# A two-layer graph network with h on the stationary side in layer two: the mean joins the product on VectorE, and TensorE transposes the sum

## The chip, the cores and the metric

The kernel runs on one core of one Trainium2 chip. The metric is the device time of one execution in microseconds (us). Engines are called by their names or as the profile does: TensorE (PE for matmuls, PEld for its weight loads), VectorE (DVE), ScalarE (ACT), GpSimd (POOL) and SyncE (SP), which only starts transfers here.

## The reference, cut to what matters

There are 12,500 nodes with 256 features each and 200,000 edges, sorted by their destination `dst`.

```python
def _sage_conv(x, src, dst, W_l, b_l, W_r):
    msgs = x[src]
    agg = segment_sum(msgs, dst, num_segments=N_NODES)
    deg = segment_sum(ones, dst, num_segments=N_NODES)
    mean = agg / maximum(deg, 1.0)[:, None]
    return mean @ W_l + b_l + x @ W_r

h = relu(_sage_conv(x, src, dst, W1_l, b1, W1_r))
h = relu(_sage_conv(h, src, dst, W2_l, b2, W2_r))
x = layernorm(x + (h @ W3 + b3))
```

## The kernel before, in words

The destinations are cut into 100 **windows** of 125 nodes (`WN`), and the edges into blocks of 128, four blocks to a **group**. Because the product with `W_l` is linear, layer one ends by writing `z = h @ W2_l` to HBM (`z_dram`), and layer two sums rows of z instead of rows of h. It also writes h itself, transposed, one window to a piece of 128 partitions by 250 columns (`h_dram`).

In each layer GpSimd runs through 304 groups. For each it starts four gathers (line 429, 128 rows of 256 numbers each) into one of the four slots of `ring`. It may overwrite a slot once TensorE has read the first three blocks of the group that lay there four groups ago (`s_gr`), and for the fourth gather once the third block of the next group has been read. VectorE marks for each group which of its 128 edges of a block belong to which node of the window (`oh`, line 940), and TensorE multiplies marks by rows (line 516), four blocks to a **pair**, into one of three banks of `psA`. VectorE adds the result two pairs later into `acc` (line 918). A group whose edges reach into a second window takes one more pair. Five heavy windows get part of their edges by another way: their counts are multiplied by all rows in order (`dense_step`, line 587), and VectorE adds that sum once in four groups (`add_hot`, line 1040), which I call the hot addition.

Behind the second and the fourth group of each four, `finish_one` lets each engine close one window i of layer two if its edges are done. Each engine comes to that place in its own program:

- VectorE, `dense2(i)`: scales the sum to the mean (line 1106), loads a register for the next window, computes one reciprocal for the norm of an earlier window (line 1100), and goes on to the next group's marks.
- TensorE, `dense2(i)`: first `product3(i)`, which is the output product of window i-1 (lines 664 and 666), then for each half m of 128 columns the two products of the weights W2_r with the transposed h (line 678, the weights stationary, h moving with 125 columns) and on top of them the transposed mean, made by a product with the identity (line 682), both in `psT`.
- ScalarE, `relu_t(i)`: waits for that, takes bias and relu into `tT` (line 1283); then `norm(i-2)` (line 1314) and `center(i-1)` (lines 1303 to 1308), and the transfers of x and h for later windows.

The order of all work is written out by hand in each engine's program; semaphores alone tie the engines together. `s_T2` counts TensorE's finished windows, `s_t2` VectorE's means, `s_tc2` ScalarE's.

The last three windows close together at the end (`finish`), behind the last group.

Of the kernel before, what the change touches and what calls it, by code (L numbers as in the profile page):

```python
# [22 lines left out]
N, E, D = 12500, 200000, 256  # L23
P = 128
WN = 125
NW = N // WN
# [121 lines left out]
def build(nc, x, src, dst, W1l, b1, W1r, W2l, b2, W2r, W3, b3, c_f, c_s, c_win, c_node, out):  # L148
# [5 lines left out]
    with ExitStack() as ctx:  # L154
# [6 lines left out]
        def sem(name):  # L161
            return ctx.enter_context(nc.semaphore(name))
# [21 lines left out]
        xt, mean, zb, sq, y = (work[:, a:a + n] for a, n in (  # L184
            (0, 2 * D), (2 * D, D), (3 * D, 2 * D), (6 * D, D), (7 * D, D)))
# [19 lines left out]
        psH, psZ = psY[:, 0:512], psY[:, 512:]  # L205
        psS = ps4[:, 2 * 512:].rearrange("p (k n) -> p k n", k=2)
# [70 lines left out]
        s_hd, s_hx = sem("s_hd"), sem("s_hx")  # L277

        s_x2, s_t2, s_T2, s_tc2, s_M3, s_y, s_act, s_sd, s_rs, s_o = (
            sem(n) for n in ("s_x2", "s_t2", "s_T2", "s_tc2", "s_M3", "s_y", "s_act", "s_sd", "s_rs", "s_o"))  # L280
# [154 lines left out]
        def _(pe):  # L435
# [234 lines left out]
            def dense2(i):  # L670
                with pe.If(i > 0):
                    product3(i)
                q = pe.snap((i & 1) * 2 * WN)
                pe.wait_ge(s_hx, i * 16 + 16)
                pe.wait_ge(s_tc2, i + 1)
                for m in range(2):
                    for k in range(2):
                        pe.matmul(psT[:, m * WN:(m + 1) * WN], w2[:, k, D + m * P:D + (m + 1) * P],  # L678
                                  hT[:, bass.ds(q + k * WN, WN)], start=(k == 0), stop=False)
                    if m == 0:  # L680
                        pe.wait_ge(s_t2, i + 1)
                    mm = pe.matmul(psT[:, m * WN:(m + 1) * WN], mean[0:WN, m * P:(m + 1) * P],  # L682
                                   ident[0:WN, 0:WN], start=False, stop=True)
                mm.then_inc(s_T2, 1)
# [78 lines left out]
        def _(v):  # L763
# [338 lines left out]
            def dense2(i):  # L1102
                at = sums()
                v.wait_ge(s_ad[1], v.snap(c, min_val=1, max_val=NG * NW + 2))
                v.wait_ge(s_T2, i + 1)
                v.tensor_scalar(mean[0:WN, :], acc[0:WN, bass.ds(at, D)],
                                rdeg[0:WN, bass.ds(i, 1)], None, ALU.mult).then_inc(s_t2, 1)
                next_range(i)
                with v.If(i > 1):
                    inverse(i)  # L1110
# [94 lines left out]
        def _(act):  # L1205
# [59 lines left out]
            def load_h(i):  # L1265
                act.dma_start(hT[:, i % 2 * 2 * WN:(i % 2 + 1) * 2 * WN], h_dram[i]).then_inc(s_hx, 16)
# [10 lines left out]

            def relu_t(i):
                act.wait_ge(s_T2, credit[s_T2] + i + 1)
                if i >= 1:  # L1280
                    act.wait_ge(s_M3, i)
                for m in range(2):
                    ins = act.activation(tT[:, m, :], psT[:, m * WN:(m + 1) * WN], ACT.Relu, bias=b2c[:, m:m + 1])  # L1283
                ins.then_inc(s_tc2, 1)
                if i + 2 < NW:
                    act.wait_ge(s_hx, 16 * (i + 2))
                    load_h(i + 2)
# [8 lines left out]
            def center(j):  # L1296
# [6 lines left out]
                link(act.activation(sq[0:WN, :], py, ACT.Copy, accum_out=sm[0:WN, 0:1]))  # L1303
# [3 lines left out]
                link(act.activation(sq[0:WN, :], y[0:WN, :], ACT.Square, accum_out=var[0:WN, :]))  # L1307
                act.activation(sd[0:WN, :], var[0:WN, :], ACT.Sqrt, bias=eps[0:WN, :], scale=1.0 / D).then_inc(s_sd, 1)

            def norm(j):  # L1310
                act.wait_ge(s_rs, j + 1)
                if j >= 2:
                    act.wait_ge(s_od[j % 2], 16 * (j // 2))
# [11 lines left out]
            act.wait_ge(s_hx, 16)  # L1325
            load_h(1)
            for i in range(NW + 2):
# [33 lines left out]
```

## Time and profile before

| | |
|---|---|
| median of 3 runs | 3268.58 us (3262.19 to 3272.46) |
| span of the profiled execution | 3265.6 us |
| PE, PEld busy | 2761.8 us (85%), 2310.7 us (71%) |
| DVE, ACT, POOL busy | 1460.5 us (45%), 498.3 us (15%), 2381.1 us (73%) |
| layer two, first to last gather | 1685.94 to 3239.04 us |

The span runs from the first to the last instruction of one execution; the page gives no other time for that execution, and the median lies 3.0 us above its span. Busy shares say how much of the span an engine computed; GpSimd's share leaves out the time in which it issues a gather. The matmul ends are modelled, so one matmul's duration in a group is longer than the step from one to the next.

### The profile page before, as it was taken

The numbers are of one execution on the slowest core, as the hardware profiler recorded it, in microseconds if no ns is written. First come the engines' busy times: TensorE is split into PE (matmuls) and PEld (weight loads), VectorE is DVE, ScalarE is ACT, GpSimd is POOL, SyncE is SP. The second block draws the span as 40 slices with busy tenths as digits, with TensorE's granted clock in tenths as the row PEclk, the third lists the DMA queues.
The fourth block names the chain that finished last, engine by engine and source line by source line (L and its number), as shares of the span: only waits on it lengthen the run. The fifth ranks groups of instructions, "written<-read, shape, count | busy, mean of one in ns | idle before, by whom it ended". The sixth has DMA issues, their size and how long they took to land.

```text
span 3265.6 us, 61269 instructions
## 1 busy us (share of the span) xinstructions
PE 2761.8 (85%) x13183; PEld 2310.7 (71%) x13184; DVE 1460.5 (45%) x3301; ACT 498.3 (15%) x1511; POOL 2381.1 (73%) x2439
## 2 busy tenths in 40 slices
PE   4888889899899899889867778878988978978877
PEld 3556778787787788678755667767777867867765
DVE  5676656666555555433333333333333333333332
ACT  2000111110110111011110121112122112212113
POOL 4757777777777777767747777777777777777775
PEclk7989999999999999899988889999989999999998
DMA  4334678587687677777755657757757757757743
GB/s 115 116 118 147 177 246 253 173 254 248 182 254 234 205 245 239 238 234 218 212 174 173 190 169 227 222 166 227 222 170 228 227 167 222 230 168 227 218 128 108
DMA packets 495815, 650.77 MB, mean 199 GB/s; under 512 B 184190, under 2 KB 414453, under 8 KB 492502
## 3 DMA queue, kind: packets, MB, share of 16 engines
q0 software_dynamic: 116736, 318.92, 32.7%
q1 hardware_dynamic: 298166, 253.95, 25.4%
q10 hardware_dynamic: 80800, 76.82, 7.8%
q14 instruction: 95, 0.78, 0.1%
q8 instruction: 18, 0.29, 0.0%
HBM read 579.07 MB, written 70.40 MB: 199 GB/s over the span
## 4 chain that ended last, share of the span: by engine, by line
PE 32%; POOL 28%; issue 17%; DVEq 9%; DMA 7%; DVE 5%; ACT 1%; SPq 1%; ACTq 0%; PEldq 0%; PEld 0%; POOLq 0%
POOL ring L429 28%; PE ps L516 19%; PE ps L587 5%; DMA ring<-z_rows,scol 4%; PE psY L631 2%; DMA ring<-in_x,scol 2%; DVEq L928 2%; PE psY L620 1%; PE psB L561 1%; DVE oh L986 1%; DVE acc L918 1%; PE psY L664 1%; DVE oh L940 1%; PE psT L678 1%; DVEq L948 1%
## 5 line engine op out<-in xcount | busy, mean ns | idle before, releaser
L516 PE MATMUL ps<-ring,oh 128*125 128x257 f32 (+1 forms) x6384 | 1606.2, 404 | 370.5 <-DMA ring<-z_rows,scol 185.7
L516 PEld LDWEIGHTS ps<-ring,oh 128*125 128x125 f32 x6384 | 1237.4, 199 | 650.0 <-issue 455.6
L429 POOL DMA_INDIRECT ring<-in_x,scol x1216 | 1196.8, 984 | 461.0 <-issue 348.4
L429 POOL DMA_INDIRECT ring<-z_rows,scol x1216 | 1183.8, 973 | 397.3 <-issue 356.0
L940 DVE SCALAR_TENSOR_TENSOR oh<-dcol,cf,iota 128x500 f32<-128x500 int16 x798 | 591.6, 741 | 630.5 <-issue 315.0
L918 DVE TENSOR_TENSOR acc<-ps,acc x802 | 338.5, 422 | 589.7 <-PE ps L516 404.7
L587 PE MATMUL ps<-scratch 128*125 128x257 f32 (+1 forms) x2000 | 476.5, 385 | 7.9 <-DMA scratch<-counts 4.8
L587 PEld LDWEIGHTS ps<-scratch 128*125 128x125 f32 x2000 | 454.2, 294 | 22.4 <-issue 6.6
L1283 ACT ACTIVATE work<-psT,b2c 128x125 f32<-128x125 f32 x200 | 62.2, 363 | 1194.1 <-PE psT L682 1194.1
L1247 ACT COPY work<-psY 125x256 f32<-125x256 f32 x100 | 37.2, 372 | 1273.6 <-PE psY L620 1273.6
L561 PE MATMUL psB<-oh 128*128 (+1 forms) x546 | 159.8, 393 | 63.8 <-DVE oh L986 60.4
L631 PEld LDWEIGHTS psY<-work,w 128*128 128x128 f32 x1600 | 198.8, 195 | 7.2 <-issue 1.1
L986 DVE TENSOR_SCALAR oh<-iota,cf,key 128x500 int16 (+1 forms) x546 | 202.0, 411 | 0.0
L631 PE MATMUL psY<-work,w 128*128 128x125 f32 x1600 | 198.3, 278 | 0.8 <-issue 0.8
L561 PEld LDWEIGHTS psB<-oh 128*128 (+1 forms) x546 | 50.8, 97 | 150.8 <-issue 118.6
L620 PE MATMUL psY<-w,hT 128*125 128x256 f32 x400 | 112.2, 405 | 14.6 <-issue 13.0
L1024 DVE COPY scratch<-psB 128x500 f32 x125 | 84.9, 679 | 82.5 <-issue 77.7
L678 PE MATMUL psT<-hT,w 128*128 x800 | 121.7, 274 | 0.1
L983 DVE TENSOR_TENSOR oh<-iota,key 128x256 int16 (+1 forms) x273 | 114.1, 418 | 9.6 <-PE psB L561 7.3
L678 PEld LDWEIGHTS psT<-hT,w 128*128 128x128 f32 x800 | 113.1, 191 | 6.5 <-issue 0.5
L664 PE MATMUL psY<-w,work 128*125 128x256 f32 x400 | 107.5, 392 | 3.1 <-ACT work L1283 2.6
L620 PEld LDWEIGHTS psY<-w,hT 128*125 128x125 f32 x400 | 74.8, 197 | 43.8 <-issue 28.1
(120 smaller groups left out, 1100.5 us busy)
## 6 DMA issues: line engine op xcount, KB each, us to landing
scratch<-counts SPq DMA_DIRECT2D x200, 312.5 KB
scratch<-in_x SPq DMA_DIRECT2D x114, 512.0 KB
scratch<-z_rows SPq DMA_DIRECT2D x114, 512.0 KB
counts<-scratch SPq DMA_DIRECT2D x25, 1250.0 KB, 8.8
work<-in_x ACTq DMA_DIRECT2D x200, 125.0 KB
ring<-in_x,scol POOLq DMA_INDIRECT x1216
ring<-z_rows,scol POOLq DMA_INDIRECT x1216
scratch<-in_x SPq DMA_DIRECT2D x114, 128.0 KB
```

What stands on the lines that cost most here:

```text
L429: pool.indirect_dma_start(ring[:, slot, b, 0:D], None, rows_dram, bass.IndirectOffsetOnAxis(scol[:, n - C0:n - C0 + 1], 0)).then_inc(rows[ ...
L516: mm = pe.matmul(psA[0:WN, bass.ds(bank, W)], oh[:, R if later else slot, b, :], ring[:, slot, b, 0:W], start=(b == 0), stop=(b == nb - 1))
L561: mm = pe.matmul(psB[:, 0:n], oh1[:, bass.ds(at, P)], oh1[:, bass.ds(at + P, n)], start=first and b == 0, stop=True, skip_group_check=True)
L587: mm = pe.matmul(psD[0:WN, 0:W], lin_a[:, q, :, :, k].rearrange("p f n -> p (f n)"), lin_x[:, q, k, 0:W], start=(q == 0 and k == 0), stop= ...
L620: mm = pe.matmul(psZ[0:WN, 0:D], hT[:, k * WN:(k + 1) * WN], w2[:, k, 0:D], start=(k == 0), stop=(k == 1))
L631: mm = pe.matmul(psH[:, m * WN:(m + 1) * WN], w1[:, a, k, m * P:(m + 1) * P], tT[:, 2 * a + k, :], start=(a == 0 and k == 0), stop=(a == 1 ...
L664: pe.matmul(at, tT[:, k, :], w3[:, k, :], start=(k == 0), stop=False)
L678: pe.matmul(psT[:, m * WN:(m + 1) * WN], w2[:, k, D + m * P:D + (m + 1) * P], hT[:, bass.ds(q + k * WN, WN)], start=(k == 0), stop=False)
L918: v.tensor_tensor(at, psA[0:WN, bass.ds(v.snap(par, min_val=0, max_val=(BANKS - 1) * 512), W)], at, ALU.add).then_inc(s_ad[l], 1)
L940: v.scalar_tensor_tensor(out=ohf[:, at:at + nb * WN].rearrange("p (b n) -> p b n", n=WN), in0=dcol[:, bass.ds(blk, nb)].unsqueeze(2).to_br ...
L983: v.tensor_tensor(s[:, :, 0:P], iota[:, 0:P].unsqueeze(1).to_broadcast([P, 2, P]), key[:, 0, bass.ds(at, 2)].unsqueeze(2).to_broadcast([P, ...
L986: ins = v.tensor_scalar(s[:, b, P:P + n], iota[:, table:table + n], base, key[:, 1, bass.ds(at + b, 1)], ALU.add, ALU.is_equal)
```

## The change

Layer two no longer streams h through stationary weights. ScalarE copies window i's h from `hT` into the free half of `tT` (`copy_h`), TensorE takes that copy as the stationary side of a product 256 columns wide, the result of which (125 nodes by 256 columns, `psU`) lies in the bank `psB`, VectorE computes acc times 1/deg plus psU in one instruction, and TensorE transposes this sum in its two halves. The scratch tile `sq` goes, since its place is now used by the copy of h; its two users write to `y` and `zb`.

```diff
+        psU = psB[0:WN, 0:D]
...
             def dense2(i):
+                pe.wait_ge(s_hc, i + 1)
+                for k in range(2):
+                    mm = pe.matmul(psU, tT[:, 2 + k, :], w2[:, k, D:2 * D], start=(k == 0), stop=(k == 1))
+                mm.then_inc(s_U, 1)
                 with pe.If(i > 0):
                     product3(i)
-                q = pe.snap((i & 1) * 2 * WN)
-                pe.wait_ge(s_hx, i * 16 + 16)
                 pe.wait_ge(s_tc2, i + 1)
+                pe.wait_ge(s_t2, i + 1)
                 for m in range(2):
-                    for k in range(2):
-                        pe.matmul(psT[:, m * WN:(m + 1) * WN], w2[:, k, D + m * P:D + (m + 1) * P],
-                                  hT[:, bass.ds(q + k * WN, WN)], start=(k == 0), stop=False)
-                    if m == 0:
-                        pe.wait_ge(s_t2, i + 1)
-                    mm = pe.matmul(psT[:, m * WN:(m + 1) * WN], mean[0:WN, m * P:(m + 1) * P],
-                                   ident[0:WN, 0:WN], start=False, stop=True)
+                    mm = pe.transpose(psT[:, m * WN:(m + 1) * WN], mean[0:WN, m * P:(m + 1) * P], ident[0:WN, 0:WN])
                 mm.then_inc(s_T2, 1)
...
                 v.wait_ge(s_T2, i + 1)
-                v.tensor_scalar(mean[0:WN, :], acc[0:WN, bass.ds(at, D)],
-                                rdeg[0:WN, bass.ds(i, 1)], None, ALU.mult).then_inc(s_t2, 1)
+                v.wait_ge(s_U, i + 1)
+                v.scalar_tensor_tensor(out=mean[0:WN, :], in0=acc[0:WN, bass.ds(at, D)],
+                                       scalar=rdeg[0:WN, bass.ds(i, 1)], in1=psU, op0=ALU.mult,
+                                       op1=ALU.add).then_inc(s_t2, 1)
                 next_range(i)
...
+            def copy_h(i):
+                act.wait_ge(s_hx[i % 2], 16 * (i // 2 + 1))
+                if i >= 1:
+                    act.wait_ge(s_U, i)
+                act.copy(tT[:, 2:4, :].rearrange("p a n -> p (a n)"),
+                         hT[:, i % 2 * 2 * WN:(i % 2 + 1) * 2 * WN]).then_inc(s_hc, 1)
+                if i + 2 < NW:
+                    act.wait_ge(s_hc, i + 1)
+                    load_h(i + 2)
+
             def relu_t(i):
+                if i + 1 < NW:
+                    copy_h(i + 1)
                 act.wait_ge(s_T2, credit[s_T2] + i + 1)
...
                 ins.then_inc(s_tc2, 1)
-                if i + 2 < NW:
-                    act.wait_ge(s_hx, 16 * (i + 2))
-                    load_h(i + 2)
...
-                link(act.activation(sq[0:WN, :], py, ACT.Copy, accum_out=sm[0:WN, 0:1]))
+                link(act.activation(y[0:WN, :], py, ACT.Copy, accum_out=sm[0:WN, 0:1]))
...
-                link(act.activation(sq[0:WN, :], y[0:WN, :], ACT.Square, accum_out=var[0:WN, :]))
+                if j >= 2:
+                    act.wait_ge(s_od[j % 2], 16 * (j // 2))
+                link(act.activation(zb[0:WN, (j % 2) * D:(j % 2 + 1) * D], y[0:WN, :], ACT.Square,
+                                    accum_out=var[0:WN, :]))
```

On TensorE, this is one window's place in layer two before the change, from the last matmul of `product3` on. Every row is one instruction or several alike; `work` holds the mean and `tT`, `w` the weights, and what stands in brackets are the semaphores waited for.

```order
L666 MATMUL psY<-work,cf 125x256
L671 UNCONDITIONAL_BRANCH
L674 ISA
L675 REGISTER_ALU [waits s_hx]
L678 REGISTER_ALU [waits s_tc2]
L678 ISA
L678 MATMUL psT<-hT,w 128x125
L678 ISA
L678 MATMUL psT<-hT,w 128x125
L682 MATMUL psT<-cf,work 128x125 [waits s_t2]
L678 MATMUL psT<-hT,w 128x125 x2
L682 MATMUL psT<-cf,work 128x125
```

The same place after the change (its line 675 is the new product, 666 and 668 are `product3`, 682 the transposes):

```order
L675 MATMUL psB<-w,work 125x256 [waits s_hc]
L675 MATMUL psB<-w,work 125x256
L677 COMPARE_AND_BRANCH
L666 REGISTER_ALU [waits s_y,s_tc2]
L666 ISA
L666 MATMUL psY<-w,work 125x256 x2
L667 REGISTER_ALU
L668 ISA [waits s_x2]
L668 MATMUL psY<-work,cf 125x256
L677 UNCONDITIONAL_BRANCH
L682 MATMUL psT<-cf,work 128x125 [waits s_t2,s_tc2]
L682 MATMUL psT<-cf,work 128x125
```

The product with h has moved ahead of `product3`, and what follows `product3` is now two transposes that wait for VectorE.

On VectorE, the same window before the change, from the wait for the last addition to the reciprocal:

```order
L1105 REGISTER_ALU [waits s_ad1]
L1106 ISA [waits s_T2]
L1106 TENSOR_SCALAR work<-acc,rdeg 125x256
L1079 ISA
L1079 TENSOR_LOAD tables
L1109 COMPARE_AND_BRANCH
L1100 REGISTER_ALU [waits s_sd]
```

And after it:

```order
L1104 REGISTER_ALU [waits s_ad1]
L1106 ISA [waits s_U,s_T2]
L1106 SCALAR_TENSOR_TENSOR work<-acc,rdeg,psB 125x256
L1078 ISA
L1078 TENSOR_LOAD tables
L1110 COMPARE_AND_BRANCH
L1099 REGISTER_ALU [waits s_sd]
```

Nothing has moved here, but the instruction now waits for TensorE's product of the same window, and the reciprocal, the hot addition and the next marks stand behind it.

On ScalarE, one window early in layer two before the change, from the relu to the first instruction of `center`:

```order
L1283 ACTIVATE work<-psT,b2c 128x125 [waits s_M3,s_T2]
L1283 ACTIVATE work<-psT,b2c 128x125
L1266 DMA hT<-h_cols 128x250 [waits s_hx]
L1212 DMA work<-in_x 125x256 [waits s_x2,s_M3]
L1303 ACTIVATE work,sm<-psY 125x256
```

And after it (1283 is now the copy, 1267 the load of h, 1296 the relu, 1313 in `center`):

```order
L1283 COPY work<-hT 128x250 [waits s_U,s_hx0]
L1267 DMA hT<-h_cols 128x250 [waits s_hc]
L1296 ACTIVATE work<-psT,b2c 128x125 [waits s_M3,s_T2]
L1296 ACTIVATE work<-psT,b2c 128x125
L1213 DMA work<-in_x 125x256 [waits s_x2,s_M3]
L1313 ACTIVATE work,sm<-psY 125x256
```

The load of h has moved from behind the relu to ahead of it, behind the new copy.

## Rows read from the trace of the kernel before

**Rows 1.** The page's first line: the span of the profiled execution.
```profile
span 3265.6 us, 61269 instructions
...
```

**Rows 2.** Groups by line, layer two (1700 to 3266 us): busy us, mean ns, idle before.
```profile
...
L429 POOL DMA_INDIRECT ring<-z_rows,scol x1205 | 1173.0, 973 | 367.2 <-issue 352.9 <-PE ps L516 14.3
L516 PE MATMUL ps<-ring,oh 128*125 128x256 f32 x3186 | 821.1, 411 | 254.7 <-DMA ring<-z_rows,scol 170.8 <-DVE oh L940 40.9 <-DVE acc L918 31.0
...
L682 PE MATMUL psT<-cf,work 125*128 125x125 f32 x400 | 77.3, 275 | 0.0
...
L1314 ACT ACTIVATE work<-work,rs 125x256 f32<-125x256 f32 x100 | 50.6, 506 | 0.5 <-DVE rs L1100 0.5
...
L1106 DVE TENSOR_SCALAR work<-acc,rdeg 125x256 f32 x100 | 37.0, 370 | 83.1 <-PE psT L682 53.0 <-DVE acc L918 29.6 <-issue 0.5
...
```

**Rows 3.** Who waited for whom, 1700 to 3240 us: total, times, longest.
```profile
...
PE ps L516 <- DMA ring<-z_rows,scol: 170.8, 74, 5.8
...
PE ps L516 <- DVE oh L940: 40.9, 20, 4.8
...
POOL ring L429 <- PE ps L516: 14.3, 47, 0.3
...
```

**Rows 4.** The gathers of layer two by their line: duration ns min/median/max, first and last start.
```profile
...
L429 POOL DMA_INDIRECT ring<-z_rows,scol x1205: 942/947/1459, 1700.1 to 3239.0; - x173
...
```

**Rows 5.** Timeline of TensorE at window 32: start us, us, instructions.
```profile
...
2245.80 1.02 PE L664 MATMUL psY<-w,work 128*125 128x256 f32 x4
...
2247.09 0.60 PE L678 MATMUL psT<-hT,w 128*128 x4
...
2248.43 1.90 PE L516 MATMUL ps<-ring,oh 128*125 128x256 f32 x8
...
```

**Rows 6.** Timeline of VectorE at the same place.
```profile
...
2241.41 0.42 DVE L1106 TENSOR_SCALAR work<-acc,rdeg 125x256 f32 x1 [0.47 <-DVE acc L918]
...
2246.05 0.74 DVE L940 SCALAR_TENSOR_TENSOR oh<-dcol,cf,iota 128x500 f32<-128x500 int16 x1 [1.09 <-PE ps L516]
...
```

**Rows 7.** Timeline of VectorE: a window with no hot addition behind it.
```profile
...
2308.31 0.35 DVE L1106 TENSOR_SCALAR work<-acc,rdeg 125x256 f32 x1 [0.26 <-DVE acc L918]
...
2310.08 0.74 DVE L940 SCALAR_TENSOR_TENSOR oh<-dcol,cf,iota 128x500 f32<-128x500 int16 x1 [0.64 <-PE ps L516]
...
```

**Rows 8.** Timeline of VectorE: a window with a hot addition (L1040) behind it.
```profile
...
2323.43 0.35 DVE L1106 TENSOR_SCALAR work<-acc,rdeg 125x256 f32 x1 [0.47 <-DVE acc L918]
...
2324.89 0.42 DVE L1040 TENSOR_TENSOR acc<-ps,acc 125x256 f32 x1 [0.33 <-PE ps L587]
2326.41 0.74 DVE L940 SCALAR_TENSOR_TENSOR oh<-dcol,cf,iota 128x500 f32<-128x500 int16 x1 [1.09 <-PE ps L516]
...
```

**Rows 9.** Timeline of TensorE from window 31 to the next wait for rows.
```profile
...
2235.80 1.02 PE L664 MATMUL psY<-w,work 128*125 128x256 f32 x4
...
2264.05 1.07 PE L664 MATMUL psY<-w,work 128*125 128x256 f32 x4
...
2266.82 1.99 PE L516 MATMUL ps<-ring,oh 128*125 128x256 f32 x8
...
```


**Rows 10.** Timeline of TensorE and GpSimd just behind it.
```profile
...
2276.83 0.95 POOL L429 DMA_INDIRECT ring<-z_rows,scol  x1 [0.30 <-issue]
...
2278.90 1.64 PE L516 MATMUL ps<-ring,oh 128*125 128x256 f32 x3 [5.38 <-DMA ring<-z_rows,scol]
...
```

**Rows 11.** Layer one's transposes of the mean and of x, whole span.
```profile
...
L646 PE MATMUL psT<-cf,work 125*128 125x125 f32 x400 | 59.6, 271 | 4.4 <-DMA work<-in_x 3.3 <-DVE work L1090 1.0
...
```

**Rows 12.** Timeline of the tail, behind the last gather.
```profile
...
3247.01 0.39 PE L682 MATMUL psT<-cf,work 125*128 125x125 f32 x2
3247.44 0.37 ACT L1283 ACTIVATE work<-psT,b2c 128x125 f32<-128x125 f32 x1 [11.91 <-PE psT L682]
...
3247.57 0.35 DVE L1106 TENSOR_SCALAR work<-acc,rdeg 125x256 f32 x1 [2.46 <-PE psT L682]
...
3251.24 0.62 ACT L1283 ACTIVATE work<-psT,b2c 128x125 f32<-128x125 f32 x2
...
```

More of the change, by code:

```diff
@@ L183, in build @@
         work = sb("work", [P, 8 * D])
-        xt, mean, zb, sq, y = (work[:, a:a + n] for a, n in (
-            (0, 2 * D), (2 * D, D), (3 * D, 2 * D), (6 * D, D), (7 * D, D)))
+        xt, mean, zb, y = (work[:, a:a + n] for a, n in (
+            (0, 2 * D), (2 * D, D), (3 * D, 2 * D), (7 * D, D)))
         tT = work[:, 5 * D:5 * D + 4 * WN].rearrange("p (a n) -> p a n", a=4)
@@ L276, in build @@
         s_zd = [sem("s_zd0"), sem("s_zd1")]
-        s_hd, s_hx = sem("s_hd"), sem("s_hx")
-        s_x2, s_t2, s_T2, s_tc2, s_M3, s_y, s_act, s_sd, s_rs, s_o = (
-            sem(n) for n in ("s_x2", "s_t2", "s_T2", "s_tc2", "s_M3", "s_y", "s_act", "s_sd", "s_rs", "s_o"))
+        s_hd, s_hc = sem("s_hd"), sem("s_hc")
+        s_hx = [sem("s_hx0"), sem("s_hx1")]
+        s_x2, s_U, s_t2, s_T2, s_tc2, s_M3, s_y, s_act, s_sd, s_rs, s_o = (
+            sem(n) for n in ("s_x2", "s_U", "s_t2", "s_T2", "s_tc2", "s_M3", "s_y", "s_act", "s_sd", "s_rs", "s_o"))
         s_od = [sem("s_od0"), sem("s_od1")]
@@ L1265, in load_h @@
             def load_h(i):
-                act.dma_start(hT[:, i % 2 * 2 * WN:(i % 2 + 1) * 2 * WN], h_dram[i]).then_inc(s_hx, 16)
+                act.dma_start(hT[:, i % 2 * 2 * WN:(i % 2 + 1) * 2 * WN], h_dram[i]).then_inc(s_hx[i % 2], 16)
             for i in range(NW + 2):
@@ L1311, in norm @@
                 act.wait_ge(s_rs, j + 1)
-                if j >= 2:
-                    act.wait_ge(s_od[j % 2], 16 * (j // 2))
                 act.activation(zb[0:WN, (j % 2) * D:(j % 2 + 1) * D], y[0:WN, :], ACT.Copy,
@@ L1324, in _ @@
             load_x(1, 1, s_x2)
-            act.wait_ge(s_hx, 16)
             load_h(1)
+            copy_h(0)
             for i in range(NW + 2):
```

## The prediction

> **What bounds the kernel now.** I read first the groups of layer two, since the change leaves layer one alone. GpSimd's 1205 recorded gathers (of 1216) are busy for 1173.0 us and "idle" before them for 367.2 us, of which 352.9 us are its own issuing [rows 2]: one gather takes 0.947 us (median), rarely up to 1.459 [rows 4], and about 0.30 us pass before the next [rows 10]. 1216 times (0.973 + 0.30) is 1548 us, and from the first to the last gather it is 1553.1 us (the table above). So GpSimd's own pace is the length of layer two. Next, the waits: GpSimd's waits for TensorE are 47 of at most 0.3 us, 14.3 us in all [rows 3], and 0.3 us is what it spends before any gather, so TensorE never held it. TensorE in turn waited 74 times for gathered rows, 170.8 us in all [rows 3]. TensorE therefore has about 11% of room here, and work taken from it in the middle of layer two comes back as a longer wait for rows. Only what holds GpSimd, or what comes behind the last gather at 3239.0 [rows 4], can move the end.
>
> **The change, part by part.**
>
> *TensorE's work.* From the start of `product3` to the next pair a window takes 2.63 us, of which the products of h and the mean are 1.34 us (2248.43 - 2247.09) [rows 5]. The new product is two matmuls of 256 columns; by the four records of L664, which is the same shape, it ends 1.02 us after its start and frees the engine after 0.86 us (2247.09 - 2245.80 is 1.29 us for three such matmuls, so 0.43 each) [rows 5]. A true transpose makes one record where a product with the identity makes two: L646 has 400 records for layer one's 400 transposes [rows 11], L682 400 for 200 [rows 2]. With 1.34 us for twelve records, 0.11 each, the two transposes take 0.22 us. TensorE does 1.08 instead of 1.34 us, 0.26 us less per window, 26 us in all, none of it on the path.
>
> *VectorE's new wait.* This is the part that counts. Before, VectorE scaled window 32's mean at 2241.41, 4.4 us before TensorE began the window at 2245.80 [rows 5, 6]; it ran ahead and had the next marks ready early. Now it waits for a product that TensorE starts only when it comes to the window. Take TensorE's start as 0. The product ends at 1.02; TensorE to VectorE takes 0.17 us (3247.40 to 3247.57) [rows 12]; so VectorE starts at 1.19. Reading PSUM and adding, its instruction is the shape of an L918 addition rather than of the 0.370 us scaling [rows 2]; I add 0.05 us. TensorE's transposes can start at 1.6 and are not due before 2.15, when `product3` is through: no wait there. But behind that instruction on VectorE are a register load, a reciprocal and the next marks. In an ordinary window the marks end 2.51 us after the scaling's start (2310.82 - 2308.31) [rows 7]; where a hot addition stands between, 3.72 us (2327.15 - 2323.43) [rows 8]. The marks are ready at 3.75 and 4.96. With 0.15 us to TensorE (my choice between nothing and the 0.5 us that an issue can take) the next pair starts at 3.9 and 5.1, where before it started at 2.63 whenever its rows lay there. By order of the program 62 windows are of the first kind, 35 of the second, and three close in the tail. The loss is 1.3 and 2.5 us, 168 us in all; less where TensorE would have waited for rows anyway. I took that off window by window from the start of each next pair, which leaves about 115 us of new lateness against 170.8 us of waits for rows [rows 3]. On average it fits; the reciprocal's old waits for ScalarE vanish beside it.
>
> *Where it does not fit.* Windows come unevenly. Between 2235.80 and 2266.82 four follow each other with no wait for rows at their end [rows 9], two of each kind: 7.6 us of lateness, with the 0.9 us of the window before them and 0.7 us for a group of two pairs, whose second marks come late too, 9.2 us. The pair at 2266.82 has read its third block 1.6 us later, at 2268.4 [rows 9]; GpSimd needs this for its gather at 2276.83 [rows 10], 8.4 us of slack. Late by 7.6 to 9.2 us it holds GpSimd for 0 to 1 us; then TensorE's wait of 5.38 us for rows [rows 10] lets all of it go. Carrying lateness forward in this way through the 304 groups, with each start as in rows like these, GpSimd is held some ten times, 11 us in all. The sum is steep: with 0.2 us less per window it is 3 us, with 0.2 more 20, with 0.4 more 31. My two guesses (0.15 and 0.05 us) are each worth that, so these are its bounds.
>
> *ScalarE's copy* of 250 columns lies between nothing and the 0.506 us of L1314, a copy of 256 columns from SBUF to SBUF [rows 2]. In the run it hides: it waits for the new product and ends while TensorE does `product3`. The load of h stays two windows ahead. Behind the last gather windows follow every 3.80 us (3247.44 to 3251.24) [rows 12], and ScalarE is what they wait for. There the copy for window 99 stands in its way, +0.45 us, and TensorE reaches the first transposes 0.26 us sooner: +0.2 us for the tail, between -0.3 and +0.8. The extra wait for an output store in `center` asks for a store two windows old: nothing. The scratch tile's move costs nothing, the instructions keep their shapes.
>
> **Sum.** 11 + 0.2 us on the profiled execution's span of 3265.6 [rows 1] gives 3276.8; its median stands 3.0 us above, so I forecast 3280 us against 3268.58, 0.34% slower.
>
> A rule that speaks against the transposes: the 400 records of L646 in layer one ran at 0.271 us each [rows 11], like L682's 0.275 [rows 2], so at the same clock. The Trainium skill says ("TensorE: Matmul & The Clock Gate", PE-mode transpose) that transposes don't count as activity for the clock gate. By the row the clock costs nothing; by the rule and VectorE's new gaps together it is rival three.
>
> **The rivals.**
>
> 1. *The new wait fits everywhere* (0.26). For it: 55 us of room is left on average, and my step from mark to matmul may be too long. Then the middle keeps GpSimd's pace and the result is 3269 us, within 0.3%. It decides at about 0.2 us less per window than I took. Against it: four windows in a row already use 7.6 of 8.4 us of slack.
> 2. *The lateness is larger than worked out* (0.12). A second pair in the next group needs its marks one by one, 0.7 us each time; at 0.4 us more per window the holds are 31 us: 3300 us.
> 3. *TensorE's clock falls more often* (0.07). TensorE's gaps change place. If 5% more of layer two ran at the lower level of 1.2 GHz, where matmuls take twice their time, that is some 39 us more work (half of 78) on a TensorE with 55 us of room left; with the unevenness above I give 3310 us.
> 4. *Faster* (0.05). Gathers longer than the median cost (973 - 947) ns times 1216, 32 us [rows 2, 4]. If these come from VectorE's work beside them, and its new position keeps the marks of line 940 out of GpSimd's way while the lateness fits, a third of it would come back: 3258 us; it decides from 10 us on. Against it: all marks remain, and GpSimd issues without a gap in which they could lie. The Trainium skill ("GPSIMD Engine Reference", Key points) names VectorE's instructions with two SBUF inputs as such neighbours; the changed instruction has one SBUF tensor and one in PSUM, so by it nothing changes here.
>
> **How the numbers follow.** A measurement of this kernel tells 0.3% (10 us) from no change. The likeliest case, holds of 3 to 31 us in the middle, has 0.50; its own range is 3272 to 3300, and 0.12 of it lies within 0.3%. With rivals two and three slower has 0.38 + 0.12 + 0.07 = 0.57; with rival one same has 0.38, and faster 0.05. The range is from rival one with the spread of the runs, 3264, to the upper bound of the holds and some spread, 3304.
>
> **What would show it.** In the profile of the changed kernel: the scaling (L1106) waits on TensorE in nearly every window, some 2 to 6 us each; the next marks start 1.8 (or 3) us after it; TensorE's waits for marks grow from 40.9 us [rows 3] to well over 100, and its waits for rows fall from 170.8 to about 60; GpSimd shows waits for TensorE longer than 0.3 us, about ten of 0.5 to 3 us. The transposes make 200 records, the new product 400. Windows in the tail stay 3.8 us apart, the last with 4.2. The prediction is wrong if the last gather still starts within 3 us of 3239 (then rival one), if TensorE waits for ScalarE's copy in the middle, or if layer one's length differs.

## The result, and the profile after

The changed kernel takes 3288.5 us in the median (3279.41 to 3290.53, 4 runs), the kernel before 3266.59 us beside it (3262.19 to 3272.46, 4 runs). The ratio is 1.0054, with a 95% interval of 1.0039 to 1.0069 (the quotient of the two medians, 1.0067, lies inside it): slower by half a per cent. The profiled execution is the fastest of the four, 3279.41 us with a span of 3277.6 us; the other three lie 9 to 11 us above it.

The page's head, after:

```profile
span 3277.6 us, 59869 instructions
## 1 busy us (share of the span) xinstructions
PE 2731.8 (83%) x12583; PEld 2265.7 (69%) x12584; DVE 1466.1 (45%) x3301; ACT 537.3 (16%) x1611; POOL 2379.9 (73%) x2439
...
```

The groups of layer two after the change (1700 to 3278 us), which answer to [rows 2]. L431 are now the gathers, L518 the products of marks and rows, L939 the marks, L1283 the copy of h, L675 the new product:

```profile
...
L431 POOL DMA_INDIRECT ring<-z_rows,scol x1207 | 1175.7, 974 | 377.4 <-issue 352.7 <-PE ps L518 24.7
L518 PE MATMUL ps<-ring,oh 128*125 128x256 f32 x3192 | 816.4, 409 | 309.8 <-DVE oh L939 210.7 <-DMA ring<-z_rows,scol 79.5 <-DVE acc L917 17.4
...
L939 DVE SCALAR_TENSOR_TENSOR oh<-dcol,cf,iota 128x500 f32<-128x500 int16 x396 | 293.5, 741 | 228.1 <-issue 147.9 <-PE ps L518 75.9
...
L675 PE MATMUL psB<-w,work 128*125 128x256 f32 x400 | 105.1, 386 | 1.6 <-ACT work L1283 1.3 <-issue 0.3
...
L1106 DVE SCALAR_TENSOR_TENSOR work<-acc,rdeg,psB 125x256 f32<-125x256 f32 x100 | 48.1, 481 | 525.9 <-PE psB L675 525.4 <-DVE acc L917 0.5
...
L1283 ACT COPY work<-hT 128x250 f32<-128x250 f32 x99 | 39.6, 400 | 1053.0 <-PE psB L675 1053.0
...
L682 PE MATMUL psT<-cf,work 125*128 125x125 f32 x200 | 37.8, 270 | 0.9 <-DVE work L1106 0.9
...
```

TensorE does less: its busy time is 2731.8 us, 30.0 less than before. GpSimd's gathers are as long as ever, 974 against 973 ns. What grew is the idle time before VectorE's sum (L1106), from 83.1 us to 525.9, and before GpSimd's gathers, where the part that waits for TensorE went from 14.3 to 24.7 us.

Who waited for whom in layer two, as in [rows 3] (engine and line that waited, what for; total, times, longest, in us):

```profile
...
DVE work L1106 <- PE psB L675: 525.4, 99, 10.8
...
PE ps L518 <- DVE oh L939: 210.7, 113, 3.6
...
PE ps L518 <- DMA ring<-z_rows,scol: 79.5, 28, 15.3
...
POOL ring L431 <- PE ps L518: 24.7, 49, 2.8
...
PE psT L682 <- DVE work L1106: 0.9, 1, 0.9
...
```

The sum now waits for TensorE in 99 of 100 windows. TensorE waits for marks for 210.7 us (40.9 before). It waits for rows for 79.5 us, and 15.3 us of this is one wait at the start of layer two, which the 170.8 us of [rows 3] leave out; like for like it is 64.2 against 170.8. On average one wait was exchanged for another; where windows lie close together there was too little of the second to exchange. GpSimd has waits of up to 2.8 us where it had none above 0.3. Since 0.3 us is what it spends before any gather, its 49 waits are 24.7 - 49 x 0.3 = 10.0 us of true holding; I call this sum the **holds**. The gathers by their line, as in [rows 4]:

```profile
...
L431 POOL DMA_INDIRECT ring<-z_rows,scol x1216: 940/946/1459, 1687.8 to 3251.3; - x174
...
```

From the first gather to the last layer two takes 1563.5 us, 10.4 more than before, and that is the holds. The last 1.9 us of the spans' difference of 12.0 come from layer one, which the change leaves alone; the tail is 0.3 us shorter.

One window on TensorE, as in [rows 5]:

```profile
...
2252.53 1.02 PE L675 MATMUL psB<-w,work 128*125 128x256 f32 x4
2253.39 1.03 PE L666 MATMUL psY<-w,work 128*125 128x256 f32 x4
2254.25 0.60 PE L668 MATMUL psY<-work,cf 126*125 x2
2254.69 0.38 PE L682 MATMUL psT<-cf,work 125*128 125x125 f32 x2
2257.66 1.99 PE L518 MATMUL ps<-ring,oh 128*125 128x256 f32 x8 [2.60 <-DVE oh L939]
...
```

And on VectorE, as in [rows 6] and [rows 8] (in brackets the idle time before, and what ended it):

```profile
...
2253.79 0.48 DVE L1106 SCALAR_TENSOR_TENSOR work<-acc,rdeg,psB 125x256 f32<-125x256 f32 x1 [5.41 <-PE psB L675]
2254.76 0.16 DVE L1099 RECIPROCAL rs<-sd 125x1 f32 x1 [0.49 <-issue]
2255.26 0.42 DVE L1039 TENSOR_TENSOR acc<-ps,acc 125x256 f32 x1 [0.33 <-issue]
2256.78 0.74 DVE L939 SCALAR_TENSOR_TENSOR oh<-dcol,cf,iota 128x500 f32<-128x500 int16 x1 [1.10 <-issue]
...
```

From the start of TensorE's product at 2252.53 it is 1.26 us to VectorE's sum, the sum takes 0.48, and a hot addition and the marks stand behind it; they end at 2257.52, and the next pair starts at 2257.66, 5.13 us after the product's start. TensorE was through with the transposes at 2255.07 and sat idle for 2.60 us. In the median the next pair follows at 3.97 us (62 ordinary windows) or 5.15 us (35 with a hot addition); before, it was 2.63 us where nothing was waited for, and 2.93 and 2.82 us in the median. Summed over the 97 windows the way from the window's start to the next pair is 120 us longer, and 10 us of that reach GpSimd. The transposes are not what waits: L682 lost 0.9 us once, in the first window.

GpSimd, from 2256 us on (gathers held by TensorE):

```profile
...
2259.49 0.95 POOL L431 DMA_INDIRECT ring<-z_rows,scol  x1 [1.15 <-PE ps L518]
...
2265.12 0.94 POOL L431 DMA_INDIRECT ring<-z_rows,scol  x1 [0.93 <-PE ps L518]
...
2270.86 0.94 POOL L431 DMA_INDIRECT ring<-z_rows,scol  x1 [1.05 <-PE ps L518]
...
2282.83 0.94 POOL L431 DMA_INDIRECT ring<-z_rows,scol  x1 [2.26 <-PE ps L518]
...
```

This is the stretch of windows that the prediction picked out by [rows 9] and [rows 10]: four waits of 1.15, 0.93, 1.05 and 2.26 us, 4.2 us of them above the 0.3 us that each gather costs anyway. The prediction had 0 to 1 us here. The other holds lie near 2510, 2757 and 2821 us: eight waits in all are longer than 0.5 us.

The tail on ScalarE, as in [rows 12] (relus at L1296, the last copy at L1283):

```profile
...
3259.24 0.62 ACT L1296 ACTIVATE work<-psT,b2c 128x125 f32<-128x125 f32 x2 [1.06 <-PE psT L682]
...
3262.99 0.38 ACT L1283 COPY work<-hT 128x250 f32<-128x250 f32 x1
3263.28 0.61 ACT L1296 ACTIVATE work<-psT,b2c 128x125 f32<-128x125 f32 x2
...
3267.02 0.60 ACT L1296 ACTIVATE work<-psT,b2c 128x125 f32<-128x125 f32 x2
...
```

The last relus follow each other at 4.04 and 3.74 us instead of 3.80 and 3.85: the copy costs 0.24 us there, and about half of it is given back at the next step.

### The profile page after: what moved, and what is told of

Same layout as the page of the kernel before. It is cut to its first block, busy times and chain, and to the rows that moved or that the text cites. A ratio compares the mean times of both kernels' runs of the same rounds, so it can differ in the third digit from the quotient of the medians.

```text
span 3277.6 us, 59869 instructions
## 1 busy us (share of the span) xinstructions
PE 2731.8 (83%) x12583; PEld 2265.7 (69%) x12584; DVE 1466.1 (45%) x3301; ACT 537.3 (16%) x1611; POOL 2379.9 (73%) x2439
## 3 DMA queue, kind: packets, MB, share of 16 engines
q0 software_dynamic: 116736, 318.92, 32.6%
## 4 chain that ended last, share of the span: by engine, by line
PE 45%; POOL 17%; issue 14%; DVEq 10%; DVE 7%; DMA 5%; SPq 1%; ACT 0%; PEld 0%; PEldq 0%; ACTq 0%; POOLq 0%
PE ps L518 28%; POOL ring L431 17%; PE ps L589 9%; PE psY L633 3%; DVE oh L939 2%; PE psB L675 2%; DMA ring<-in_x,scol 2%; DMA ring<-z_rows,scol 2%; DVEq L1078 2%; PE psY L622 2%; DVEq L927 2%; PE psB L563 1%; DVE oh L985 1%; DVE acc L917 1%; DVEq L939 1%
## 5 line engine op out<-in xcount | busy, mean ns | idle before, releaser
L518 PE MATMUL ps<-ring,oh 128*125 128x257 f32 (+1 forms) x6384 | 1599.0, 403 | 417.6 <-DVE oh L939 247.9
L518 PEld LDWEIGHTS ps<-ring,oh 128*125 128x125 f32 x6384 | 1232.6, 198 | 696.5 <-issue 503.8
L431 POOL DMA_INDIRECT ring<-in_x,scol x1216 | 1194.7, 982 | 464.8 <-issue 350.7
L431 POOL DMA_INDIRECT ring<-z_rows,scol x1216 | 1184.6, 974 | 407.1 <-issue 355.2
L939 DVE SCALAR_TENSOR_TENSOR oh<-dcol,cf,iota 128x500 f32<-128x500 int16 x798 | 591.2, 741 | 523.1 <-issue 335.4
L1106 DVE SCALAR_TENSOR_TENSOR work<-acc,rdeg,psB 125x256 f32<-125x256 f32 x100 | 48.1, 481 | 525.9 <-PE psB L675 525.4
L1283 ACT COPY work<-hT 128x250 f32<-128x250 f32 x100 | 40.0, 400 | 1060.6 <-PE psB L675 1053.0
L622 PE MATMUL psY<-w,hT 128*125 128x256 f32 x400 | 111.9, 404 | 13.9 <-issue 12.2
L1023 DVE COPY scratch<-psB 128x500 f32 x125 | 84.8, 679 | 83.1 <-issue 76.9
L675 PE MATMUL psB<-w,work 128*125 128x256 f32 x400 | 105.1, 386 | 1.6 <-ACT work L1283 1.3
```

Source lines behind the costliest of these rows:

```text
L431: pool.indirect_dma_start(ring[:, slot, b, 0:D], None, rows_dram, bass.IndirectOffsetOnAxis(scol[:, n - C0:n - C0 + 1], 0)).then_inc(rows[ ...
L518: mm = pe.matmul(psA[0:WN, bass.ds(bank, W)], oh[:, R if later else slot, b, :], ring[:, slot, b, 0:W], start=(b == 0), stop=(b == nb - 1))
L622: mm = pe.matmul(psZ[0:WN, 0:D], hT[:, k * WN:(k + 1) * WN], w2[:, k, 0:D], start=(k == 0), stop=(k == 1))
L675: mm = pe.matmul(psU, tT[:, 2 + k, :], w2[:, k, D:2 * D], start=(k == 0), stop=(k == 1))
L939: v.scalar_tensor_tensor(out=ohf[:, at:at + nb * WN].rearrange("p (b n) -> p b n", n=WN), in0=dcol[:, bass.ds(blk, nb)].unsqueeze(2).to_br ...
```

## The experiments

All medians are of several runs of the kernel and of the kernel before on the same chip. The theory to test, in short: the loss is VectorE's new wait for a product that TensorE starts late; it delays the next marks, these the next pair, and where windows lie close together that holds GpSimd. Against it stands that the loss comes from something else in the change: the transposes and TensorE's clock, TensorE's other work, ScalarE's copy.

### ahead: the same product, one window early

TensorE computes window i+1's product at the end of window i, so that VectorE finds it ready. All else of the change stays.

```diff
-            def dense2(i):
-                pe.wait_ge(s_hc, i + 1)
+            def product_h(n):
+                pe.wait_ge(s_hc, n)
                 for k in range(2):
                     mm = pe.matmul(psU, tT[:, 2 + k, :], w2[:, k, D:2 * D], start=(k == 0), stop=(k == 1))
                 mm.then_inc(s_U, 1)
+
+            def dense2(i):
+                with pe.If(i < 1):
+                    product_h(1)
                 with pe.If(i > 0):
                     product3(i)
...
                 mm.then_inc(s_T2, 1)
+                with pe.If(i < NW - 1):
+                    product_h(i + 2)
```

> The changed kernel with one thing moved: TensorE computes the product of h for window i+1 at the end of window i's place, behind the transposes, instead of at the start of its own place (window 0's stays where it is). Every instruction of the change remains. Theory one (VectorE's wait for that product makes the next marks late, the ring's slack is used up and GpSimd is held): VectorE no longer waits there, the holds go, and the time is that of the kernel before, 3267 us within 5. Theory two (the cost lies in the operations themselves: ScalarE's copy, the new product's bank, the addition from PSUM): the time stays that of the changed kernel, 3283 to 3290.

Measured: 3268.24 us (12 runs) against 3268.52, ratio 0.9991 [0.9979, 1.0002]. The waits of its layer two:

```profile
...
PE ps L518 <- DMA ring<-z_rows,scol: 186.1, 81, 15.2
...
DVE work L1112 <- PE psB L675: 62.6, 33, 8.6
PE ps L518 <- DVE oh L945: 60.8, 29, 4.6
...
POOL ring L431 <- PE ps L518: 12.2, 40, 0.3
...
```

The waits stand near [rows 3] again (of the 186.1 us for rows, 15.2 are the wait at the start), the next pair follows 2.38 us after `product3`'s start where nothing is waited for, and the holds are 12.2 - 40 x 0.3 = 0.2 us. With the product's place alone the whole loss is gone, while copy, product, sum and transposes are all still there. What the change does apart from that wait costs nothing that can be measured.

### wait_only: the wait, without the change

The kernel before, with its old products and its scaling, but VectorE's scaling waits until TensorE has done the two w3 matmuls of `product3` in the same window. No work is added or taken.

```diff
...
                 for k in range(2):
-                    pe.matmul(at, tT[:, k, :], w3[:, k, :], start=(k == 0), stop=False)
+                    mm = pe.matmul(at, tT[:, k, :], w3[:, k, :], start=(k == 0), stop=False)
+                mm.then_inc(s_q, 1)
...
                 v.wait_ge(s_T2, i + 1)
+                v.wait_ge(s_q, i + 1)
                 v.tensor_scalar(mean[0:WN, :], acc[0:WN, bass.ds(at, D)],
                                 rdeg[0:WN, bass.ds(i, 1)], None, ALU.mult).then_inc(s_t2, 1)
```

> The kernel before with the wait alone: VectorE's scaling of window i's mean now also waits for the second matmul of product3(i), which ends 1.02 us after TensorE starts the window, as the new product does in the changed kernel. No operation is added or taken. Theory one: as slow as the changed kernel or a little less (the scaling is 0.05 to 0.1 us shorter than the new sum), 3278 to 3290 us, with holds of GpSimd of 8 to 20 us. Theory two: 3267 us as before.

Measured: 3280.84 us (12 runs) against 3268.52, ratio 1.0040 [1.0027, 1.0053]. Its waits in layer two:

```profile
...
DVE work L1108 <- PE psY L664: 518.2, 99, 10.4
...
PE ps L516 <- DVE oh L941: 174.3, 111, 3.6
...
PE ps L516 <- DMA ring<-z_rows,scol: 74.7, 27, 14.5
...
POOL ring L429 <- PE ps L516: 19.6, 48, 1.2
...
```

These are nearly the rows of the changed kernel, and the next pair follows at 3.94 and 5.15 us, as there. The wait alone, put on the old kernel, gives 12.3 us of loss in the median. The holds in its profile are only 5.2 us, below the 8 to 20 that I expected. The profile's span is 12.8 us over that of the kernel before: 4.7 us of it lie between the first and the last gather of layer two, 2.7 behind the last gather (29.3 instead of 26.6 us), and 5.3 ahead of the first, in layer one, which the edit leaves alone. There the profiles of these runs differ by up to 7.7 us (the first gather of layer two starts between 1683.5 and 1691.2 us), so the total of one profile says little about a few microseconds; what lengthens the part behind the last gather the runs don't show.

### late: the same product, behind product3

```diff
             def dense2(i):
+                with pe.If(i > 0):
+                    product3(i)
                 pe.wait_ge(s_hc, i + 1)
                 for k in range(2):
                     mm = pe.matmul(psU, tT[:, 2 + k, :], w2[:, k, D:2 * D], start=(k == 0), stop=(k == 1))
                 mm.then_inc(s_U, 1)
-                with pe.If(i > 0):
-                    product3(i)
```

> The changed kernel with the product of h behind product3 instead of ahead of it, so that VectorE is let go 1.29 us later in each window. Theory one: carried forward through the groups, 1.29 us more per window gives some 94 us of holds instead of 11: 3330 to 3385 us. Theory two: the same operations, so 3283 to 3290 us.

Measured: 3411.54 us (4 runs), ratio 1.0437 [1.0418, 1.0456]. Two of its waits:

```profile
...
POOL ring L431 <- PE ps L518: 170.0, 103, 6.8
...
PE psT L682 <- DVE work L1106: 86.8, 100, 0.9
...
```

The transposes, which come right behind the product here, wait for VectorE's sum as well, 0.87 us a window. The next pair follows at 5.23 and 6.44 us, 1.3 us later than in the changed kernel, and the holds are 170.0 - 103 x 0.3 = 139.1 us. That is 129 us more than in the changed kernel, for 97 x 1.3 = 126 us of new lateness. The sign and the steepness are as expected, the size is beyond it: carrying the lateness forward had given holds of 94 us, and I expected 3330 to 3385 us. Lateness need not be all of it, since TensorE's clock differs too. From first to last gather, the changed kernel first, then `late`:

```profile
...
1688.00:3251.00 1563.00, 1257.09 (x5334) 1058.67 (x5335) 534.21 (x1080) 325.64 (x1060) 1183.42 (x1215) 0.94 0.65 196
...
```

```profile
...
1686.00:3374.00 1688.00, 1332.83 (x5317) 1095.88 (x5318) 532.95 (x1075) 325.54 (x1060) 1179.91 (x1213) 0.90 0.61 181
...
```

TensorE (first column behind the length of the stretch) is busy for 76 us longer with nearly the same number of matmuls, at a granted clock of 0.90 instead of 0.94 (third value from the end). How much of the 129 us comes from that is not shown. The median is 143.0 us over the kernel before.

### ident: products with the identity in place of the transposes

```diff
-                    mm = pe.transpose(psT[:, m * WN:(m + 1) * WN], mean[0:WN, m * P:(m + 1) * P], ident[0:WN, 0:WN])
+                    mm = pe.matmul(psT[:, m * WN:(m + 1) * WN], mean[0:WN, m * P:(m + 1) * P],
+                                   ident[0:WN, 0:WN], start=True, stop=True)
```

> The changed kernel with the two transposes made again as products with the identity, two records each instead of one, 0.2 us more of TensorE's work in each window. Theory one: that work ends at 2.6 us after TensorE's start, before the next marks at 3.9, so it hides: the same as the changed kernel, 3283 to 3290 us. Theory three (what counts is how long TensorE works at each window): 0.2 us per window, on the steep part of the sum, costs 5 to 10 us more: 3293 to 3300 us. If the clock gate ignored transposes and this mattered, the granted clock would be higher here than 0.945.

Measured: 3280.91 us (12 runs), ratio 1.0031 [1.0020, 1.0042], and the changed kernel's is 1.0043 [1.0028, 1.0059] in the comparison below: the intervals overlap. Its granted clock over the span is 0.943, with transposes it is 0.946 and 0.949 in two profiles, and before the change 0.941. The rule of the Trainium skill that the prediction weighed ("TensorE: Matmul & The Clock Gate", PE-mode transpose) would have a lower clock with the transposes; these numbers show none. The next pair follows at 3.96 and 5.15 us, the holds are 11.4 us.

### after_again and recip_first: the changed kernel, and with the reciprocal moved

The second takes the reciprocal out of the way between the sum and the marks: VectorE computes it before it waits.

```diff
             def dense2(i):
+                with v.If(i > 1):
+                    inverse(i)
                 at = sums()
...
                 next_range(i)
-                with v.If(i > 1):
-                    inverse(i)
```

> The changed kernel itself, unchanged, beside the others on one chip: 3280 to 3290 us, with about 10 us of holds of GpSimd in layer two (waits for TensorE beyond the 0.3 us of every gather).

> The changed kernel with VectorE's reciprocal for the norm computed ahead of the wait for the product of h instead of behind the sum. The wait and all operations stay; only the way from the wait to the next marks is shorter, by 0.5 to 0.8 us per window. Theory one: carried forward, 0.4 us less per window leaves no hold, so 3267 to 3271 us, with VectorE still waiting some 500 us for TensorE. Theory two (operations): as the changed kernel, 3283 to 3290 us.

Measured, against 3270.18 us for the kernel before: the changed kernel 3281.78 us (6 runs), ratio 1.0043 [1.0028, 1.0059], and with the reciprocal moved 3276.37 us (12 runs), 1.0026 [1.0012, 1.0041]. Two waits of the latter:

```profile
...
PE ps L518 <- DVE oh L939: 168.4, 106, 3.1
...
POOL ring L431 <- PE ps L518: 19.8, 46, 2.1
...
```

The next pair comes at 3.64 and 4.83 us in the median; window by window it is 0.43 us (ordinary) and 0.32 us (hot) earlier than in the changed kernel. The holds are 19.8 - 46 x 0.3 = 6.0 us. The changed kernel's second profile has 32.6 - 58 x 0.3 = 15.2:

```profile
...
POOL ring L431 <- PE ps L518: 32.6, 58, 3.3
...
```

The changed kernel's median and its 15.2 us of holds are within what I expected. With the reciprocal moved, the medians and the holds have the expected sign, about half of the loss, but the two intervals overlap, so the gain is not shown beyond doubt: layer two is 1562.2 us long in the profile, against 1563.5 and 1569.7 in the changed kernel's two. I had expected nearly all of the loss to go, and that is a miss. The step is 0.3 to 0.4 us instead of the 0.5 to 0.8 that I named; but I had worked out "no hold" for 0.4 us, so it is the carrying forward that failed: even at this lateness GpSimd is still held.

### before_3g, after_3g, ahead_3g: GpSimd with less to do

To see how near TensorE is to being the bound, GpSimd starts three gathers a group in layer two instead of four; the data of the fourth block are left out.

```diff
-                    for b in range(GB):
+                    for b in range(GB - l):
...
-                pe.reg_mov(turn, 16 * GB)
+                pe.reg_mov(turn, 16 * (GB - l))
```

> The kernel before with three gathers per group in layer two instead of four; the fourth block of each slot keeps what layer one left there, so the output of layer two is not the reference's. GpSimd's part falls to 912 gathers of 1.27 us, 1160 us; TensorE's own work and its waits for marks, some 1390 us of the 1553 us from first to last gather, become the length of layer two: 3090 to 3120 us. If GpSimd were not the bound before, the time would fall by less than 60 us.

> The changed kernel with three gathers per group in layer two (same data left out). Theory one: where TensorE sets the pace nothing absorbs the late marks, so nearly the whole 168 us of lateness shows against before_3g, less 0 to 20 us: 3240 to 3280 us. Theory two: as much slower than before_3g as the changed kernel is than the kernel before, 15 to 20 us. If TensorE's saved 0.26 us per window counted, it would be 26 us faster than before_3g.

> The kernel with the product of h one window ahead, with three gathers per group in layer two (the fourth block's data left out as in before_3g). Theory one: with VectorE's wait gone and TensorE nearly the bound, TensorE's saved 0.26 us per window shows: 26 us faster than before_3g's 2959.7, 2930 to 2950 us, against after_3g's 3162. Theory two (operations): near after_3g.

Measured (3 runs each): before_3g 2959.74 us, ratio 0.9049 [0.9027, 0.9070]; after_3g 3162.03 us, 0.9676 [0.9658, 0.9694]; ahead_3g 2935.20 us against 3275.39, 0.8967 [0.8946, 0.8988]. The absolute ranges of the first two were too high, `ahead_3g` lies in its own, which was given after the first two had run. Of before_3g the waits of layer two, and 500 us in its middle (busy us and instructions of each engine, then TensorE's granted clock):

```profile
...
POOL ring L429 <- PE ps L516: 91.7, 96, 2.6
...
PE ps L516 <- DMA ring<-z_rows,scol: 36.1, 17, 13.2
...
```

```profile
...
core 0: us, PE busy (x) PEld busy (x) DVE busy (x) ACT busy (x) POOL busy (x), PEclk, DMA share, GB/s
...
2200.00:2700.00 500.00, 490.92 (x2491) 442.88 (x2490) 210.30 (x423) 121.74 (x410) 357.01 (x364) 1.00 0.73 220
...
```

And of after_3g:

```profile
...
POOL ring L431 <- PE ps L518: 310.9, 147, 7.3
...
```

From the first to the last gather before_3g takes 1236 us, and its time is some 130 us or more below what I expected: a miss. Between 2200 and 2700 us the kernel before shows a clock of 0.94 and before_3g 1.00, and TensorE's busy time from first to last gather is 1181 us instead of 1286 (before first, then before_3g):

```profile
...
1686.00:3239.00 1553.00, 1285.68 (x5917) 1102.10 (x5918) 528.82 (x1080) 286.90 (x962) 1182.76 (x1215) 0.93 0.66 197
...
```

```profile
...
1684.00:2920.00 1236.00, 1181.36 (x5915) 1049.84 (x5916) 525.34 (x1080) 286.53 (x962) 896.09 (x911) 0.99 0.71 215
...
```

So the 170.8 us of waits for rows understate TensorE's room: 1553 against 1236 us is 20%, not 11%, a third of it from shorter busy time at the higher clock.

With that room gone the new wait costs what the windows say. after_3g lies 202 us above before_3g, 2.1 us for each of 97 windows; the next pair is late by 1.3 and 2.5 us there (3.97 and 5.14 us against 2.63), 168 us in all, and the clock in the profile is lower as well (0.951 against 0.967 over the span). And ahead_3g, with the product early, is faster than before_3g by 24.5 us. The two ran on different chips, on which the kernel before took 3270.18 and 3275.39 us; against these the step is 29.7 us, and in the two profiles layer two is 17.7 us shorter. So the size is rough, but it fits the 26 us of TensorE's work that the prediction had put at "none of it on the path": they appear as soon as TensorE's work is on the path.

### marks_psum: a third way, for the long gathers

The prediction's rival four rested on gathers longer than the median. In the kernel before 112 gathers of layer two take more than 1.0 us; above the median all gathers together cost 32.2 us. Here the kernel before gets one edit: the numbers 0 to 124, with which VectorE compares to make the marks, lie in PSUM in layer two, in the free bank `psB`.

```diff
+        iotaP = psB[:, 0:WN]
...
-                    in1=iota[:, 0:WN].unsqueeze(1).to_broadcast([P, nb, WN]),
+                    in1=(iotaP if l else iota[:, 0:WN]).unsqueeze(1).to_broadcast([P, nb, WN]),
...
+            v.tensor_copy(iotaP, iota[:, 0:WN]).then_inc(s_pi, 1)
+            v.wait_ge(s_pi, 1)
             layer(1, dense2)
```

> The kernel before, with the numbers 0 to 124 that line 940 compares with lying in PSUM (bank psB, free in layer two) instead of SBUF, in layer two only, so that the marks read one tensor from SBUF instead of two. No wait changes; each mark takes some 0.06 us more. In the kernel before, 112 of layer two's 1216 gathers took over 1.0 us, 96% of them beside a mark, 32 us over the median in all. If the marks' second SBUF tensor is what stretches them: that excess falls below 10 us and the time to 3240 to 3250 us. If only the neighbourhood counts, whatever the marks read, or something else stretches them: 112 long gathers again and 3266 to 3272 us.

Measured: 3238.26 us (6 runs, 3235.76 to 3239.73) against 3275.39, ratio 0.9888 [0.9871, 0.9905]. Its gathers by their line as in [rows 4], and the groups of gathers and marks (L942) as in [rows 2]:

```profile
...
L431 POOL DMA_INDIRECT ring<-z_rows,scol x1207: 942/947/1076, 1699.2 to 3209.8; - x173
...
```

```profile
...
L431 POOL DMA_INDIRECT ring<-z_rows,scol x1207 | 1143.9, 948 | 368.0 <-issue 357.0 <-PE ps L518 11.0
...
L942 DVE SCALAR_TENSOR_TENSOR oh<-dcol,cf,psB 128x500 f32<-128x500 f32 x396 | 290.8, 734 | 344.5 <-PE ps L518 206.6 <-issue 133.2
...
```

The longest gather is 1.076 us instead of 1.459, 9 instead of 112 are above 1.0 us, and what is above the median adds up to 0.9 us. Layer two takes 1521.9 us instead of 1553.1. The marks cost 0.734 us each; with the old operand they cost 0.741. The Trainium skill says that GpSimd and VectorE contend for SBUF where VectorE's instruction reads two SBUF inputs ("GPSIMD Engine Reference", Key points); this trace agrees, and gives the price here, 31 us. With its place the operand also changed its type, from int16 to fp32; 32-bit numbers left in SBUF were not run, so that the place does it, and not the type, is argued and not shown. This is the version that beats both kernels. Layer one was not tried, since `psB` is in use there, nor was it joined with `ahead`.

## Why the prediction was right, and where it wasn't

The forecast was 3280 us, 0.34% slower, for the case "holds of 3 to 31 us in the middle". That case came true: 0.54% slower, with holds of 10.0 us in one profile and 15.2 in another. `ahead` and `wait_only` show the cause from both sides, `late` shows that the loss grows with the lateness.

**VectorE's new wait.** Right in each link. The sum starts 1.27 us after the product (1.19 forecast), the next pair comes at 3.97 and 5.15 us (3.9 and 5.1 forecast), and the new lateness adds up to 120 us (115 forecast). Of my two guesses the step from marks to TensorE is 0.14 us (0.15 taken), and VectorE's instruction takes 0.48 us (0.42 taken). TensorE's waits for marks grew to 210.7 us ("well over 100"), its waits for rows fell to 64.2 beside the one at the start ("about 60"), and the four windows near 2260 were one of four places.

**The sum of the holds** is the term that was mis-sized. I carried lateness forward from the starts of one profile and got 11 us. The profiled execution has 10.0, but that the two agree so closely is in part luck. In the stretch that I had worked out I had 0 to 1 us of holds, at its last gather only; the trace has 4.2 us, 2.0 of them there and the rest at three gathers ahead of it. And the median lies 11.6 and 21.9 us above the kernel before in the two comparisons. The same working gives 94 us for `late`, where 139 are measured, and nearly none for `recip_first`, where it is 6. It comes out low away from the place at which it was made. In the table the next pair is the median; "layer two longer" is the time from first to last gather in the profile, above the 1553.1 us of the kernel before:

| kernel | next pair, ordinary / hot, us | holds in profile, us | layer two longer, us | median above before, us |
|---|---|---|---|---|
| before | 2.93 / 2.82 | 0.2 | 0 | 0 |
| ahead | 2.69 / 2.48 | 0.2 | -0.9 | -0.3 |
| recip_first | 3.64 / 4.83 | 6.0 | 9.1 | 6.2 |
| wait_only | 3.94 / 5.15 | 5.2 | 4.7 | 12.3 |
| ident | 3.96 / 5.15 | 11.4 | 9.8 | 12.4 |
| changed kernel | 3.97 / 5.15 | 10.0, 15.2 | 10.4, 16.6 | 21.9, 11.6 |
| late | 5.23 / 6.44 | 139.1 | 137.4 | 143.0 |

Of the bounds that I gave for it, 20 us (0.2 us more per window) does not hold the first comparison's 21.9 us; 31 us (0.4 more), on which the range rests, does. Single profiles and medians agree no better than a few microseconds here, and `wait_only`, with the same lateness, has half the holds: such a sum can be off by a factor of two. Why the first four runs lie at 3288 and the later six at 3282 the runs don't settle: the chips and the kernel before differ by some microseconds too.

**TensorE's room.** "About 11% of room" was wrong as a statement on TensorE: 170.8 us is the time in which it waits for rows at the clock that those waits leave it. before_3g shows at least 20%, for GpSimd still sets part of its pace (its holds are 91.7 - 96 x 0.3 = 62.9 us). The forecast survived because what is lost is not an average but lies where windows follow closely, and one such place was read from the timeline.

**TensorE's work and ScalarE's copy.** 200 records of transposes at 0.270 us, 400 of the product, as forecast. 26 us less work came out as 30 us of busy time, and ahead_3g shows 25 to 30 us of it when it is on the path. The busy time holds an effect of the clock as well, so the agreement of the sizes is not exact. The copy takes 0.400 us (0.45 taken) and hides. The tail was forecast 0.2 us longer and is 0.3 us shorter.

**The rivals.** One, that the wait fits everywhere, is refuted by the holds. I had put its point at 0.2 us less per window; at 0.3 to 0.4 less (`recip_first`) GpSimd is still held for 6.0 us, and the loss is 0.26%, below the 0.3% that the prediction took as telling. Two, 31 us of holds, did not come; the nearest to it are the 21.9 us of the first comparison. Three, the clock: 0.946 and 0.949 against 0.941, no fall. Four was right on its first half only: the long gathers do come from VectorE's marks, worth 31 us, but moving the marks in time did not shift them (974 against 973 ns); putting an operand into PSUM did.

## What to carry to other kernels

When one engine takes a new operand from another, ask when the producer starts it, not how long it takes: put it at the end of the step before, as `ahead` does, and the same change costs nothing. Slack between two engines is not an average; find the stretch where the tightest steps follow each other, and add the lateness there. And look at the bounding engine's own instructions for a tail above the median: the 32 us that lay in GpSimd's long gathers was larger than the 12 to 22 us that the change cost.

## What the hardware showed that I had not expected

- VectorE's marks with both tensors in SBUF stretch GpSimd's gathers from 0.947 us to as much as 1.459 us; with the one operand in PSUM the longest is 1.076 us, and the marks are not slower (0.734 us). The operand's type changed with its place, from int16 to fp32.
- TensorE's granted clock in the same 500 us (2200 to 2700 us) was 1.00 in before_3g, 0.96 after the change, 0.94 before it and 0.91 in `late`: a mix of the levels 2.4 and 1.2 GHz. TensorE's busy time in it was 490.9, 415.7, 435.9 and 402.6 us, so the clock is highest where it hardly pauses, but does not follow the busy time alone; what sets it between these is not settled. The higher clock shortens TensorE's work, by 105 us over layer two in before_3g.
- A transpose makes one record of 0.270 us, a product of 256 columns with h two matmuls of 0.43 us each, and VectorE's sum with an operand in PSUM takes 0.481 us where the scaling took 0.370.
